# Moving a per-edge matrix product from the relation stage into the convolution stage of a graph network kernel

## The chip, the cores and the metric

VectorE (DVE) and ScalarE (ACT) do elementwise work, GpSimd (POOL) issues the indirect DMAs that gather rows by index, SyncE (SP) issues plain DMAs. Each engine works through its own list in order; semaphores order the engines among one another.

## The reference, cut to what matters

There are 6250 nodes with 128 features, and 100,000 edges sorted by target `dst`. Four graph layers run one after the other, each with its own weights and each followed by a residual and a normalization. Two of them matter here. They use the same edge features `edge_attr` (100,000 x 128).

```
layer 0 (convolution):
    h   = x @ w1.T + b1
    msg = silu(h[src] + (edge_attr @ we.T + be))
    agg = segment_sum(msg, dst)
layer 3 (relation network), the first linear layer of its edge MLP, 384 -> 256:
    hidden = relu(concat(h3[dst], h3[src], edge_attr) @ re_w1 + re_b1)
    effect = segment_sum(hidden @ re_w2 + re_b2, dst)
```

The kernel splits `re_w1` in three. The products of the node features with two of the parts are tables of 6250 rows, made once. The third product is `edge_attr @ re_w1[256:384]`, a 128 -> 256 product for every edge. It depends on inputs and weights alone. `re_w2` is applied after the sum over edges, in the update stage.

## The kernel before, in words

The edges lie in tiles of 128, one edge per partition. `G` = 4 tiles make a group, and four groups (`U` = 16 tiles) a round. The convolution's edge loop (`phase_conv_edges`) makes the messages of 196 groups of tiles, and sums them over 208 groups of steps. A step is a pair of an edge tile and a node tile that it touches; there are a few more steps than tiles. The relation's edge loop (`phase_relation`, after its node part) runs over 208 groups of steps. Each order is written out by hand: `staggered` and `pipeline` call each engine's stage functions turn by turn, with fixed lags in turns, and everything between engines is a wait on a counting semaphore.

Convolution, of one group n. SP loads 4 tiles of transposed edge features (`load`, L632). POOL issues 4 indirect DMAs, each gathering 128 rows of 512 bytes (L646), into one of 4 row buffers per group, when `row_free` says that the message four groups back is made (L742). PE multiplies the edge features with `we` into one PSUM bank (`edge_product`, L664, 4 products of 128 columns, each two matmul instructions). DVE adds the rows (`message`, L738) into a ring in SBUF, ACT applies SiLU in place (L689). For the sum over edges DVE compares the numbers 0 to 127 with each edge's target column (`one_hot`, L729, 128x512), PE multiplies that matrix with the messages (`sum_into_nodes`, L679), and DVE adds the four results to the node sums one after the other (`add_sums`, L760). Per turn DVE's order is match_high (L717, each fourth turn), one_hot(n), message(n), next_idx, add_sums(n-1), count_high (L724, each fourth turn). PE's order is edge_product(n), then sum_into_nodes(n-1), which waits until message(n) is made. Here `lane`, the row of numbers 0 to 127, is a copy in PSUM bank 7.

Relation, of one group n. SP loads 4 tiles of edge features again (L1583, 64 KB each) and the broadcast target columns (L1580). POOL gathers 4 times 128 rows of 1 KB (L1596). ACT makes the transposed one-hots in two steps, |rel - p| and then relu(1 - that) (`distance` L1647, `is_nought` L1654). PE accumulates two products in PSUM for each tile (`hidden_product`): edge features by `re_w1`'s third part (L1618) and one-hot by node table (L1619), 256 columns each. DVE adds the gathered rows in two halves (`add_rows`, L1710), ACT applies ReLU (`act`, L1659, 128x1024), DVE makes the one-hots for the sum (`sum_matrix`, L1699, two instructions of 128x256), PE sums (`sum_into_nodes`, L1630, 256 columns), DVE adds to the node sums (`add_sums`, L1731), and DVE casts the next indices (`stage`, L1670). `sum_matrix` of group n waits on `spread` until sum_into_nodes(n-2) has read that buffer of `oh`.

Of the kernel before, what the change touches and what calls it, by code (L numbers as in the profile page):

```python
# [21 lines left out]
F32 = mybir.dt.float32  # L22
# [582 lines left out]
def phase_conv_edges(nc, k, table, agg, room):  # L605

    with ExitStack() as c:
# [5 lines left out]
        ea = room[:, (RING + U) * D:(RING + 2 * U) * D].rearrange("p (j e) -> p j e", e=G * P)  # L613
        oh = sb("oh", [P, 2, G, P], F32)
        ea_in = [sem(f"ea_in{j}") for j in range(GROUPS)]
        row_in = k.row_in
        ea_free, row_free, idx_ready, pool_turn = sem("ea_free"), sem("row_free"), sem("idx_ready"), sem("pool_turn")
# [7 lines left out]
        lane, lane_set = k.psum[:, 7, 0:P], sem("lane_set")  # L625
        of_ring = lambda j: ring[:, G * j:G * j + G, :]
        with nc.Block() as block:
            @block.sync
            def _(sp):
                def load(i, j):  # L630
                    sp.wait_ge(ea_free, PER * i + j + 1)
# [3 lines left out]
                staggered(PER, (load, 0, TILE_GROUPS))  # L635
# [17 lines left out]
            def _(pe):  # L653
                pe.sem_inc(ea_free, GROUPS)
                pe.sem_inc(spread, 2)
                pe.matmul(lane, k.ident[:], k.lane[:], start=True, stop=True).then_inc(lane_set, 1)
                regs = {}

                def edge_product(i, j):
                    n = PER * i + j  # L660
                    pe.wait_ge(summed, n + 1)
                    pe.wait_ge(ea_in[j % GROUPS], 16 * (TURNS * i + j // GROUPS) + 16)
                    for q in range(G):
                        mm = pe.matmul(k.psum[:, j % 2, q * D:(q + 1) * D], ea[:, j % GROUPS, q * P:(q + 1) * P],  # L664
                                       k.w["L0_gnn_wet"][:], start=True, stop=True)
                    mm.then_inc(product, 1)
                    pe.wait_ge(product, n + 1)
                    pe.sem_inc(ea_free, 1)

                def sum_into_nodes(i, j):  # L670
# [4 lines left out]
                    pe.wait_ge(summed, min(n + 4, TILE_GROUPS + 2) if isinstance(n, int) else n + 4)  # L675
                    pe.wait_ge(oh_ready, n + 1)
                    pe.wait_ge(added, G * n + G)
                    for q in range(G):
                        mm = pe.matmul(k.psum[:, 2 + j % 2, q * D:(q + 1) * D], oh[:, j % 2, q, :],  # L679
# [6 lines left out]
            def _(a):  # L686
                def act(i, j):
                    a.wait_ge(summed, PER * i + j + 3)
                    nc.scalar.activation(of_ring(j), of_ring(j), ACT.Silu).then_inc(msg_ready, 1)  # L689

                staggered(PER, (act, 0, TILE_GROUPS))

            @block.vector
            def _(v):
                v.sem_inc(summed, 2)
# [15 lines left out]

                v.wait_ge(lane_set, 1)
# [20 lines left out]
                def message(i, j):  # L733
                    n = PER * i + j
                    v.wait_ge(product, n + 1)
                    for q in range(G):
                        v.wait_ge(row_in[G * (j % GROUPS) + q], 16 * (TURNS * i + j // GROUPS) + 16)
# [1294 lines left out]
```

## Time and profile before

| | us |
|---|---|
| median of 3 runs | 5034.16 (5031.56 to 5040.16) |
| the profiled execution | 5032.72 |
| its span, first to last instruction | 5030.9 |
| mean granted TensorE clock of the span | 0.781 |
| first and last gather of the convolution's edge loop (start) | 83.0, 1074.5 |
| first and last gather of the relation's edge loop (start) | 3803.0, 4887.1 |

The span is 1.8 us shorter than the profiled execution's time. The table's last two rows place the loops that are changed; the work between them (placing and attending by source, attention heads) is not changed in the code. Matmul ends are modelled, so a PE that shows as busy all the time isn't thereby at its limit; the rate of its instruction starts tells more.

### The profile page before, as it was taken

The numbers are of one execution on the slowest core, as the hardware profiler recorded it, in microseconds if no ns is written. First come the engines' busy times: TensorE is split into PE (matmuls) and PEld (weight loads), VectorE is DVE, ScalarE is ACT, GpSimd is POOL, SyncE is SP. The second block draws the span as 40 slices with busy tenths as digits, with TensorE's granted clock in tenths as the row PEclk, the third lists the DMA queues.
The fourth block names the chain that finished last, engine by engine and source line by source line (L and its number), as shares of the span: only waits on it lengthen the run. The fifth ranks groups of instructions, "written<-read, shape, count | busy, mean of one in ns | idle before, by whom it ended". The sixth has DMA issues, their size and how long they took to land. (4 is left out here: it accounts for less than half of the span.)

```text
span 5030.9 us, 76241 instructions
## 1 busy us (share of the span) xinstructions
PE 3877.7 (77%) x19917; PEld 3472.4 (69%) x19917; DVE 2952.5 (59%) x8048; ACT 1631.2 (32%) x2985; POOL 3439.9 (68%) x3536
## 2 busy tenths in 40 slices
PE   4556555555999999996986556566559999999998
PEld 3555555554988888886765555555548888888885
DVE  6555555557433333334786667667676666666665
ACT  1111111113333333334863233323325444444442
POOL 3777777742777777777645777777755777777761
PEclk7776777766665666557997777777779999999999
DMA  4333333327333333334754444444436666666651
GB/s 122 105 103 105 103 104 104 103 67 127 105 101 102 106 101 103 100 103 136 221 156 147 129 128 130 129 128 129 129 89 187 178 178 178 178 178 179 178 152 60
DMA packets 491437, 649.05 MB, mean 129 GB/s; under 512 B 94519, under 2 KB 354059, under 8 KB 490798
## 3 DMA queue, kind: packets, MB, share of 16 engines
q0 software_dynamic: 132032, 325.99, 22.5%
q1 hardware_dynamic: 346462, 312.02, 22.4%
q10 hardware_dynamic: 12560, 6.52, 0.8%
q8 instruction: 168, 2.75, 0.2%
q14 instruction: 215, 1.76, 0.1%
HBM read 554.38 MB, written 89.82 MB: 128 GB/s over the span
## 5 line engine op out<-in xcount | busy, mean ns | idle before, releaser
L1181 POOL DMA_INDIRECT by_src<-R,p_idx x832 | 833.3, 1002 | 345.1 <-issue 224.0
L1596 POOL DMA_INDIRECT R<-table_ps,r_idx x832 | 815.6, 980 | 339.6 <-issue 210.9
L1376 POOL DMA_INDIRECT R<-table_kv,h_idx x832 | 811.4, 975 | 322.3 <-issue 297.4
L646 POOL DMA_INDIRECT R<-table,c_idx x784 | 747.2, 953 | 275.5 <-issue 236.5
L1406 PE MATMUL psum<-R,h_oh 128*128 128x137 f32 x1664 | 357.3, 378 | 417.7 <-issue 235.8
L679 PE MATMUL psum<-R,c_oh 128*128 x1664 | 333.0, 362 | 421.3 <-DVE R L738 412.7
L1406 PEld LDWEIGHTS psum<-R,h_oh 128*128 128x128 f32 x1664 | 306.7, 265 | 459.3 <-issue 457.6
L679 PEld LDWEIGHTS psum<-R,c_oh 128*128 128x128 f32 x1664 | 281.6, 255 | 472.7 <-issue 472.7
L1731 DVE TENSOR_TENSOR R<-R,psum 128x256 f32 x832 | 345.9, 416 | 379.8 <-PE psum L1630 378.7
L760 DVE TENSOR_TENSOR R<-R,psum 128x128 f32 x832 | 238.8, 287 | 466.8 <-PE psum L679 372.5
L1618 PE MATMUL psum<-w_L_gnn_re_w,r_ea 128*128 128x256 f32 x1664 | 496.0, 380 | 2.5 <-issue 2.5
L1619 PE MATMUL psum<-R 128*128 x1664 | 495.6, 379 | 0.0
L984 PE MATMUL psum<-p_src_score,R 128*128 128x50 f32 x1664 | 450.1, 363 | 54.0 <-issue 53.8
L984 PEld LDWEIGHTS psum<-p_src_score,R 128*128 128x128 f32 x1664 | 363.0, 269 | 83.7 <-issue 83.7
L1659 ACT ACTIVATE X<-X 128x1024 f32<-128x1024 f32 x208 | 219.8, 1057 | 602.4 <-DVE X L1710 602.4
L689 ACT ACTIVATE R<-R 128x512 f32<-128x512 f32 x196 | 123.4, 629 | 884.9 <-DVE R L738 884.9
L1630 PE MATMUL psum<-X,early_cols 128*128 128x256 f32 x1664 | 393.0, 379 | 2.5 <-ACT X L1659 2.5
L985 PE MATMUL psum<-R 128*128 x1664 | 388.6, 303 | 0.0
L994 PE MATMUL psum<-R 128*128 x1664 | 381.7, 422 | 0.0
L1145 DVE SCALAR_TENSOR_TENSOR R<-early_cols,src_cols 128x8 f32<-128x8 f32 x104 | 18.6, 178 | 604.4 <-ACTq L1030 604.4
L985 PEld LDWEIGHTS psum<-R 128*128 128x128 f32 x1664 | 372.1, 275 | 0.0
L994 PEld LDWEIGHTS psum<-R 128*128 128x128 f32 x1664 | 361.3, 328 | 0.0
(337 smaller groups left out, 7773.6 us busy)
## 6 DMA issues: line engine op xcount, KB each, us to landing
R<-by_src SPq DMA_DIRECT2D x220, 260.0 KB, 3.1
r_ea<-in_ea_t SPq DMA_DIRECT2D x832, 64.0 KB, 2.8
R<-in_ea_t SPq DMA_DIRECT2D x196, 256.0 KB
R<-rel_rows SPq DMA_DIRECT2D x104, 256.0 KB
R<-lo_rows SPq DMA_DIRECT2D x104, 256.0 KB, 3.8
h_rel<-rel_rows SPq DMA_DIRECT2D x208, 128.0 KB, 3.1
r_rel<-rel_rows SPq DMA_DIRECT2D x208, 128.0 KB, 3.1
by_src<-R,p_idx POOLq DMA_INDIRECT x832, 2.5
```

What stands on the lines that cost most here:

```text
L646: g.indirect_dma_start(out=rows[:, u, :], out_offset=None, in_=table, in_offset=bass.IndirectOffsetOnAxis(ap=idx[:, j // GROUPS % 2, u:u + ...
L679: mm = pe.matmul(k.psum[:, 2 + j % 2, q * D:(q + 1) * D], oh[:, j % 2, q, :], ring[:, bass.ds(regs["slot"][G * (j % GROUPS) + q], 1), :], ...
L984: pe.matmul(cols[:, 0:NT], is_lo[:, j, q * P:(q + 1) * P], src_score[:], start=True, stop=True)
L985: mm = pe.matmul(cols[:, NT:WIDE], is_rel[:, j, q * P:(q + 1) * P], H[:, bass.ds(regs["node"][G8 * j + q], 1), D + 1:D + 2], start=True, s ...
L994: mm = pe.matmul(k.psum[:, 4 + 2 * j + h, (q % G) * D:(q % G + 1) * D], is_rel[:, j, q * P:(q + 1) * P], H[:, bass.ds(regs["node"][G8 * j ...
L1181: g.indirect_dma_start(out=by_src, out_offset=bass.IndirectOffsetOnAxis(ap=idx[:, u:u + 1], axis=0), in_=rows[:, u, :], in_offset=None).th ...
L1376: g.indirect_dma_start(out=rows[:, u, :], out_offset=None, in_=table, in_offset=bass.IndirectOffsetOnAxis(ap=idx[:, u:u + 1], axis=0)).the ...
L1406: mm = pe.matmul(sums(j, q), oh[:, j % 2, q, :], msg[:, j % 2, q, :], start=True, stop=True)
L1596: g.indirect_dma_start(out=rows[:, u, :], out_offset=None, in_=table, in_offset=bass.IndirectOffsetOnAxis(ap=idx[:, u:u + 1], axis=0)).the ...
L1618: pe.matmul(hidden(j, q), ea[:, G * j + q, :], k.w["L3_gnn_re_w1"][:, 2 * HID:3 * HID], start=True, stop=False)
L1619: mm = pe.matmul(hidden(j, q), oht[:, j % 2, q * P:(q + 1) * P], Dh[:, bass.ds(regs["node"][G * j + q], 1), :], start=False, stop=True)
L1630: mm = pe.matmul(sums(j, q), oh[:, j % 2, q, :], msg[:, j % 2, q, :], start=True, stop=True)
```

## The change

The convolution's PE product gets a moving operand of 384 columns (`both`): `re_w1`'s third part and `we` side by side. Of each tile it makes 256 columns of the relation's edge product and 128 of the convolution's, in one bank. A group takes two halves of two banks, and three such pairs of banks rotate (`of_banks`); the banks 6 and 7 hold the sums, and so `lane` is now read from SBUF. DVE makes the message in two halves. ACT copies each half's 256 columns from PSUM into `part` in SBUF (`keep`), then applies SiLU. SP stores `part` to DRAM (`store`, 512 KB per group) in a new tensor `edge_part`.

The relation loads 128 KB of `edge_part` per tile in place of 64 KB of edge features. DVE adds the gathered rows to it in SBUF (`join`, two halves), and `add_rows` adds the PSUM product to that sum. PE's `hidden_product` has the one-hot product alone. `sum_matrix` moves from DVE to ACT, as four |.| of 128x128 and a relu of 128x512. The size of the scratch memory for dynamic DMAs is given as 8192 at the build, where it was left to the default.

```diff
@@ phase_conv_edges
+        both = room[:, used:used + HID + D]
+        of_banks = lambda h, cols: k.psum[:, 2 * (h % 3):2 * (h % 3) + HALF, cols]
-        lane, lane_set = k.psum[:, 7, 0:P], sem("lane_set")
+        lane = k.lane[:]
 sync:
+                def store(i, j):
+                    n = PER * i + j
+                    sp.wait_ge(kept, 2 * n + 5)
+                    sp.dma_start(k.edge_part[n * G * P:(n + 1) * G * P, :].rearrange("(q p) d -> p q d", p=P), part[:, j % GROUPS]
+                                 ).then_inc(part_out[j % GROUPS], 16)
-                staggered(PER, (load, 0, TILE_GROUPS))
+                staggered(PER, (load, 0, TILE_GROUPS), (store, GROUPS, TILE_GROUPS))
 tensor, edge_product:
-                    pe.wait_ge(summed, n + 1)
-                    for q in range(G):
-                        mm = pe.matmul(k.psum[:, j % 2, q * D:(q + 1) * D], ea[:, j % GROUPS, q * P:(q + 1) * P],
-                                       k.w["L0_gnn_wet"][:], start=True, stop=True)
+                    for h in (2 * n, 2 * n + 1):
+                        pe.wait_ge(kept, h + 1)
+                        for q in range(HALF):
+                            at = (h % 2 * HALF + q) * P
+                            mm = pe.matmul(k.psum[:, 2 * (h % 3) + q, 0:HID + D], ea[:, j % GROUPS, at:at + P], both,
+                                           start=True, stop=True)
+                        mm.then_inc(product, 1)
 scalar:
+                def keep(i, j):
+                    turn = TURNS * i + j // GROUPS
+                    if turn > 0:
+                        a.wait_ge(part_out[j % GROUPS], 16 * turn)
+                    for h in range(2):
+                        n = 2 * (PER * i + j) + h
+                        a.wait_ge(summed, n + 1)
+                        nc.scalar.copy(part[:, j % GROUPS, h * HALF:h * HALF + HALF], of_banks(n, slice(0, HID))).then_inc(kept, 1)
 vector, message:
+                    for h in (2 * n, 2 * n + 1):
+                        v.wait_ge(product, h + 1)
+                        v.tensor_tensor(of_ring(j)[:, at:at + HALF, :], of_banks(h, slice(HID, HID + D)), rows[:, u:u + HALF, :],
+                                        ALU.add).then_inc(summed, 1)
@@ phase_relation
 sync:
-                            sp.wait_ge(product, GROUPS * i + j + 1)
+                            sp.wait_ge(summed, 2 * (GROUPS * i + j) + 2)
-                        sp.dma_start(ea[:, u, :], k.ea_t[:, bass.ds(tile[u] * P, P)]).then_inc(ea_in[u], 16)
+                        sp.dma_start(part[:, u, :], k.edge_part[bass.ds(tile[u] * P, P), :]).then_inc(part_in[j], 16)
 gpsimd:
-                            g.wait_ge(summed, 2 * (GROUPS * i + u // G) + 2)
+                            g.wait_ge(joined, 2 * (GROUPS * i + u // G) + 2)
 tensor, hidden_product:
-                        pe.matmul(hidden(j, q), ea[:, G * j + q, :], k.w["L3_gnn_re_w1"][:, 2 * HID:3 * HID], start=True, stop=False)
 scalar:
+                def sum_matrix(i, j):
+                    n = GROUPS * i + j
+                    a.wait_ge(spread, n + 1)
+                    for q in range(G):
+                        at = i * U + G * j + q
+                        nc.scalar.activation(oh[:, j % 2, q, :], k.lane[:], ACT.Abs, bias=k.rel_cols[:, at:at + 1],
+                                             scale=-1.0).then_inc(sum_apart, 1)
+                    a.wait_ge(sum_apart, G * n + G)
+                    nc.scalar.activation(oh[:, j % 2], oh[:, j % 2], ACT.Relu, bias=k.ones[:, 0:1], scale=-1.0).then_inc(oh_ready, 1)
-                pipeline(ITERS, GROUPS, distance, is_nought, act, lags=(0, 1, 3))
+                pipeline(ITERS, GROUPS, distance, is_nought, sum_matrix, act, lags=(0, 1, 2, 3))
 vector:
+                def join(h):
+                    def join_half(i, j):
+                        u = G * j + 2 * h
+                        if h == 0:
+                            v.wait_ge(part_in[j], 16 * G * (i + 1))
+                        for q in range(2):
+                            v.wait_ge(row_in[u + q], 16 * i + 16 * (before + 1))
+                        v.tensor_tensor(part[:, u:u + 2, :], part[:, u:u + 2, :], rows[:, u:u + 2, :], ALU.add).then_inc(joined, 1)
+                        if h == 1:
+                            stage(i + 1, j)
+                    return join_half
-                pipeline(ITERS, GROUPS, add_sums(0), sum_matrix, add_sums(1), add_rows(0), add_sums(2),
-                         add_rows(1), add_sums(3), lags=(3, 1, 3, 1, 3, 1, 3))
+                pipeline(ITERS, GROUPS, add_sums(0), join(0), add_sums(1), join(1), add_sums(2), add_rows(0), add_sums(3),
+                         add_rows(1), lags=(3, 1, 3, 1, 3, 1, 3, 1))
@@ build
-    nc = bacc.Bacc("TRN2", target_bir_lowering=False, num_devices=1)
+    nc = bacc.Bacc("TRN2", target_bir_lowering=False, num_devices=1, dynamic_dma_scratch_size=8192)
```

## Rows read from the trace of the kernel before

**Rows 1.** Windows: busy us and instructions per engine, clock, DMA share, GB/s.
```profile
500.00:625.00 125.00, 72.70 (x387) 66.86 (x388) 67.46 (x165) 15.74 (x25) 94.83 (x100) 0.72 0.38 105
2375.00:2500.00 125.00, 113.85 (x828) 99.86 (x827) 99.59 (x311) 105.86 (x413) 85.18 (x104) 1.00 0.80 221
2875.00:3000.00 125.00, 72.80 (x397) 66.93 (x398) 87.09 (x249) 38.67 (x75) 95.32 (x98) 0.78 0.47 129
4250.00:4375.00 125.00, 125.00 (x581) 110.04 (x580) 80.47 (x216) 55.44 (x74) 95.73 (x97) 1.00 0.62 178
```

**Rows 2.** Groups of instructions, convolution, 82 to 1122: busy us, mean ns | idle before.
```profile
L646 POOL DMA_INDIRECT R<-table,c_idx x784 | 747.2, 953 | 275.5 <-issue 236.5 <-DVE c_idx L700 30.2 <-DVEq L742 8.8
...
L760 DVE TENSOR_TENSOR R<-R,psum 128x128 f32 x827 | 237.4, 287 | 465.7 <-PE psum L679 372.0 <-DVE R L760 3.7 <-issue 3.2
L729 DVE TENSOR_TENSOR c_oh<-psum,rel_cols 128x512 f32<-128x512 f32 x208 | 141.9, 682 | 0.4
L738 DVE TENSOR_TENSOR R<-psum,R 128x512 f32<-128x512 f32 x196 | 133.4, 681 | 6.9 <-DMA R<-table,c_idx 6.9
...
L724 DVE TENSOR_REDUCE count<-c_same_high 128x7 f32<-128x896 bf16 x49 | 52.9, 1080 | 0.0
```

**Rows 3.** Line L738 (message): ns min/median/max, first and last start.
```profile
L738 DVE TENSOR_TENSOR R<-psum,R x196: 674/681/693, 90.4 to 1089.8; 128x512 f32<-128x512 f32 x196
```

**Rows 4.** Line L646 (gather), and what its engine sat idle for (us, times).
```profile
L646 POOL DMA_INDIRECT R<-table,c_idx x784: 946/952/1730, 83.0 to 1074.5; - x196
...
  DVEq L742: 8.8, 27
```

**Rows 5.** Timeline, convolution, TensorE at the upper clock: start us, us.
```profile
612.52 0.68 DVE L738 TENSOR_TENSOR R<-psum,R 128x512 f32<-128x512 f32 x1
...
613.40 1.15 PE L679 MATMUL psum<-R,c_oh 128*128 x8 [2.23 <-DVE R L738]
...
614.70 1.58 DVE L760 TENSOR_TENSOR R<-R,psum 128x128 f32 x4 [1.50 <-PE psum L679]
```

**Rows 6.** Timeline, convolution, the same product at the lower clock.
```profile
603.68 2.07 PE L679 MATMUL psum<-R,c_oh 128*128 x8 [1.78 <-DVE R L738]
```

**Rows 7.** Timeline, relation, a turn in the steady stretch.
```profile
4300.56 0.68 DVE L1710 TENSOR_TENSOR X<-psum,R 128x512 f32<-128x512 f32 x1
...
4301.28 1.06 ACT L1659 ACTIVATE X<-X 128x1024 f32<-128x1024 f32 x1 [2.90 <-DVE X L1710]
4301.43 1.89 PE L1630 MATMUL psum<-X,early_cols 128*128 128x256 f32 x8
...
4302.85 0.70 ACT L1654 ACTIVATE R<-R,ones 128x512 f32<-128x512 f32 x1
...
4303.47 0.42 DVE L1731 TENSOR_TENSOR R<-R,psum 128x256 f32 x1 [1.83 <-PE psum L1630]
...
4303.81 0.76 DVE L1699 TENSOR_TENSOR early_cols<-lane,rel_cols 128x256 f32<-128x256 f32 x2
...
4304.26 1.12 POOL L1596 DMA_INDIRECT R<-table_ps,r_idx  x1 [0.30 <-issue]
...
4305.68 0.95 POOL L1596 DMA_INDIRECT R<-table_ps,r_idx  x1 [0.30 <-issue]
...
4306.41 0.41 DVE L1731 TENSOR_TENSOR R<-R,psum 128x256 f32 x1
...
4306.61 1.89 PE L1630 MATMUL psum<-X,early_cols 128*128 128x256 f32 x8
```

**Rows 8.** Groups of instructions, POOL in the heads stage, 2800 to 3700.
```profile
L1376 POOL DMA_INDIRECT R<-table_kv,h_idx x704 | 686.7, 975 | 214.5 <-issue 191.9 <-DVE h_idx L1449 22.5
```

**Rows 9.** Timeline, ACT in the attend stage: a |.| of 128x128 and its follower.
```profile
2479.72 0.39 ACT L1240 ACTIVATE a_away<-lane,R 128x128 f32<-128x128 f32 x1
2480.01 0.19 ACT L1234 ACTIVATE a_minus<-a_weight 128x1 f32<-128x1 f32 x1
```

**Rows 10.** Groups of instructions, ACT, whole span: a copy of 128x512 from PSUM.
```profile
L1033 ACT COPY R<-psum 128x512 f32<-128x512 f32 x208 | 112.8, 590 | 731.3 <-DMA by_src<-R,p_idx 607.5 <-PE psum L994 123.8
```

More of the change, by code:

```diff
@@ L613, in phase_conv_edges @@
         ea = room[:, (RING + U) * D:(RING + 2 * U) * D].rearrange("p (j e) -> p j e", e=G * P)
+        used = (RING + 2 * U) * D
+        part = room[:, used:used + GROUPS * G * HID].rearrange("p (j q d) -> p j q d", j=GROUPS, d=HID)
+        used += GROUPS * G * HID
+        both = room[:, used:used + HID + D]
+        kept, both_ready, part_out = sem("kept"), sem("both_ready"), [sem(f"part_out{j}") for j in range(GROUPS)]
+        HALF = G // 2
+        of_banks = lambda h, cols: k.psum[:, 2 * (h % 3):2 * (h % 3) + HALF, cols]
         oh = sb("oh", [P, 2, G, P], F32)
@@ L653, in _ @@
             def _(pe):
-                pe.sem_inc(ea_free, GROUPS)
                 pe.sem_inc(spread, 2)
-                pe.matmul(lane, k.ident[:], k.lane[:], start=True, stop=True).then_inc(lane_set, 1)
+                pe.wait_ge(both_ready, 2)
                 regs = {}
@@ L1551, in phase_relation @@
         oh = k.early_cols[:, 0:2 * G * P].rearrange("p (b q e) -> p b q e", b=2, q=G)
-        ea_in = [sem(f"ea_in{u}") for u in range(U)]
+        part = sb("part", [P, U, HID], F32)
+        part_in = [sem(f"part_in{j}") for j in range(GROUPS)]
+        joined, sum_apart = sem("joined"), sem("sum_apart")
         rel_in = [sem(f"rel_in{n}") for n in range(GROUPS)]
@@ L1665, in _ @@
                 v.sem_inc(summed, 2 * GROUPS)
+                v.sem_inc(joined, 2 * GROUPS)
                 v.sem_inc(spread, 2)
@@ L1694, in _ @@
                 v.wait_ge(zeroed, 1)
[L1696 to L1702 removed]
+                def join(h):
[9 more added lines that the diff above has]
+                    return join_half
                 def add_rows(h):
                     def add_half(i, j):
+                        n = GROUPS * i + j
+                        u = G * j + 2 * h
                         if h == 0:
[L1707 to L1709 removed]
+                            v.wait_ge(product, n + 1 + GROUPS)
+                        v.wait_ge(joined, 2 * (n + GROUPS) + h + 1)
                         v.tensor_tensor(msg[:, j % 2, 2 * h:2 * h + 2, :].rearrange("p q d -> p (q d)"),
                                         k.psum[:, 2 * (j % 2) + h, :],
[L1712 removed]
+                                        part[:, u:u + 2, :].rearrange("p q d -> p (q d)"),
                                         ALU.add).then_inc(summed, 1)
[L1714 to L1716 removed]
                     return add_half
```

59 lines of the change are left out of this document (22 added, 37 removed).

## The prediction

> **What bounds the kernel now.** I read first which engine is full in which stretch (busy time by windows), then each changed loop's costliest groups, then one turn of each loop in the timeline.
>
> The two loops have different bounds. In the relation TensorE's clock is granted in full and it shows as busy throughout [rows 1]. From one sum product to the next are 4306.61 - 4301.43 = 5.18 us [rows 7]. Eight instructions of 256 columns take 1.89 us to the last one's end [rows 7]; with one instruction's 0.38 us taken off, that is 1.51 / 7 = 0.216 us from start to start. A turn has 24 of them, 5.18 us. So PE is the bound there, and POOL is close behind: a gather lasts 0.95 us with 0.30 us before it, so four of them take 5.02 us, and 5.2 with the longer one of 1.12 us [rows 7].
>
> In the convolution PE is busy 73 of 125 us and POOL 95 [rows 1], which looks like a POOL bound. The loop's own rates say something finer. Messages are made every (1089.8 - 90.4) / 195 = 5.13 us [rows 3]. Gathers would go every 5.02 us by the same 0.95 + 0.30 [rows 2], and they do (1074.5 - 83.0) / 783 x 4 = 5.07 us only because POOL waits at times for a row buffer that VectorE gives back [rows 4]. At the end the last message starts 1089.8 - 1074.5 - 0.95 = 14.3 us behind the last gather. So the bound is a loop of DVE and PE: message(n), PE's sum product, four dependent additions, one-hot, message(n+1). At the upper clock the step through PE costs 1.50 us, at the lower one PE's part is 2.07 instead of 1.15 [rows 5, 6]. The mean clock is 0.72 [rows 1]. POOL is 0.1 us per group faster than this loop, no more.
>
> **Convolution, after.** PE's work grows. The new product has 384 columns, so 0.216 x 1.5 = 0.324 us per instruction, 2.6 us for the eight of a group, beside about 0.9 us for the sum. That is 3.5 of some 5.1 us. At the lower clock it would be 7.0 us, which doesn't fit, so PE would never rest and would be back at the upper one. Does the upper one hold at 68%? The attend stage has 828 instructions in 125 us at some 0.11 us each (eight of 128 columns in 1.15 us less the last one's own end [rows 5]), 73%, and shows a clock of 1.00 [rows 1]. I take 1.00.
>
> The DVE loop then is 1.50 (PE step) + 1.58 (four additions) + 0.27 (a quarter of count_high's 1.08) + 0.68 (one-hot) + 0.33 and 0.42 (the message's halves, priced as the 128x256 additions of the relation) = 4.8 us [rows 2, 5, 7]. By PE it is 0.2 + 0.9 + 2.6 + 0.2 + 0.42 = 4.3 us. Both are under POOL's 5.02, so POOL becomes the bound. ACT's two copies of 128x512 from PSUM at 0.59 [rows 10] and the SiLU make 1.8 us per group, beside everything; three pairs of banks let PE run ahead of them. The store waits on `kept`, on SP, with only a load behind it that is due three groups later; nothing waits for it but `keep` four groups on. It adds 512 KB per 5.1 us, 100 GB/s to 105. DMA share goes from 0.38 to perhaps 0.7, and 0.80 has been carried [rows 1]. Cost zero, plus some 3 us for the last stores' landing.
>
> POOL doesn't stay at 5.02, however. The one-hot now reads `lane` in SBUF, so both its inputs lie there. In the relation a gather that starts at 4304.26, under L1699 with both inputs in SBUF (4303.81 to 4304.57), lasts 1.12 us where the next takes 0.95 [rows 7]. The gather waits until that instruction ends. In the heads stage, with one such instruction of 128x512 in each group, gathers have a mean of 975 ns against 953 here [rows 2, 8]. The bounds: no hit, 5.02 us per group; a hit of the full 0.6 us in each group, 5.6. I take the heads' rate, a start every 1.28 us. The last gather starts at 83.0 + 783 x 1.28 = 1085, is done by 1086 and lands some 2 us later, so the last message starts at 1088 instead of 1089.8: -2 us. With the store +1 us. Ends: at 1.255 us it would be 83 + 983 + 3 = 1069, -21 us; at 1.40 us 1182, +92 us.
>
> The Trainium skill (SBUF — State Buffer, Who interferes with whom) has a rule for this: a VectorE instruction with two SBUF inputs contends with a GpSimd instruction that reads SBUF, and the second to issue is blocked until the first is done. The row above agrees in that the gather is the longer one. The same page infers that descriptor generation isn't held by `tensor_tensor`; by that the convolution would gain the 21 us, and the 1.12 us speaks against it.
>
> **Relation, after.** PE loses 8 of 24 instructions: 16 x 0.216 = 3.45 us per turn. POOL's floor is 5.02, DVE's turn is 4306.41 + 0.41 - 4303.47 = 3.35 us of work now [rows 7], less two halves of 128x256 (0.67) plus two joins of 128x512 (2 x 0.6): 3.9. ACT gets four |.| and a relu of 0.70. The |.| of the same form lasts 0.39 and the next instruction starts 0.29 after its start [rows 9], so four take 3 x 0.29 + 0.39 = 1.26. ACT's sum is 2 x 0.61 + 1.26 + 0.1 + 0.70 + 0.96 = 4.2 us. Each engine alone has room.
>
> What has none is a new ring. sum_matrix(n+1) on ACT waits for `spread` of sum_into_nodes(n-1). Behind it in ACT's order stands act(n), and sum_into_nodes(n) waits for act(n). Before, `sum_matrix` was on DVE; act(n), at 4301.28 to 4302.34, ended 4.3 us ahead of its product at 4306.61 [rows 7]. Now each turn has in series: PE's eight products 1.89; to ACT 0.15 (as PE to DVE, 4303.32 to 4303.47); |.| 1.26; wait for the last one 0.1; relu 0.70; act 1.06 less 0.1 of overlap; to PE 0.2: 5.26 us [rows 5, 7, 9]. That is over PE's old 5.18 and over POOL. distance and is_nought (1.3) run beside PE's 1.89, hidden_product (1.7) beside ACT's 3.0. The bounds: |.| as close as its data alone allow and no hand-over cost gives 4.9, under POOL, so 5.02 and (5.02 - 5.18) x 208 = -33 us; 0.39 each for |.| and slow hand-overs 5.6, +87 us. I take 5.26: +0.08 x 208 = +17 us. Under this ring POOL has 0.24 us per turn to spare for the joins, both of whose inputs lie in SBUF; a hit on one of four gathers costs about that much, so it is free at best just so. SP's loads double to 512 KB per turn, some 220 GB/s, at a share near 0.8; they are asked for four turns ahead, as the buffer is free after add_rows. I price them at zero.
>
> **The smaller scratch for DMAs.** No row shows its cost. The bounds are nothing and, were each of 3280 gathers and scatters held by a hundredth of a microsecond or two, some 50 us. The 0.30 between gathers is the same everywhere, and no wait for room is seen. I take zero.
>
> **Sum.** 5032.7 (this execution) + 1 + 17 = 5051 for the profiled execution. The median shown is 1.4 us above it: 5052. The first product of the convolution now stands behind two copies on ACT, and the relation's last ones behind one more |.| and relu (1.26 + 0.70): with 4 us for these, 5056. A difference of 0.2% (10 us) is about what a measurement tells from none.
>
> **Rivals.**
> A, both loops at POOL's pace without hits: the ring closes in under 5.02, one-hot and joins fall between gathers. -21 + 3 - 33 = -51 from the median: 4983. For it: each engine's sum is below 5.02 and the gather grid can lock to the DVE order. Against it: the series on ACT, and the 1.12. A half of it (one loop) gives 5015. Chance 0.28 together.
> B, the hits decide (the other side of A): in the relation two joins of 0.6 us under four gather starts give 2 x 0.6 / 5.2 x 4 = 0.9 hits of 0.3 us or more, 5.33 us; in the convolution the one-hot hits once per group, 5.3. (5.33 - 5.18) x 208 + 196 x 0.2 = +31 + 39: 5105. It decides once POOL is behind the ring, from 0.24 us of hits per turn. Chance 0.2.
> C, PE's clock falls in the new idle third: the convolution has 36% of PE's time in use at the upper clock and swings between both levels (mean 0.72). If relation and convolution came to 0.85, the ring would have 1.9 more in a third of turns: +0.6 x 208, 5180. Against it the attend stage. Chance 0.05.
> D, the ring costs just what PE cost, and the rest cancels: 5034, within 10 us. Chance 0.17. My forecast, 5056, has 0.3.
> Faster 0.29, same 0.21, slower 0.5. The range is 4990 to 5120; it leaves out the best of A and C.
>
> **What would show it.** Relation: sum products 5.26 us apart, ACT busy over 4 us a turn, ACT's idle time before sum_matrix ended by PE's sum product, and that product waiting on ACT's act; POOL waiting on the cast. If PE waits on DVE, and DVE on gathers, it is B. Convolution: message waits for rows and the lag behind the gathers stays near 2 us; gathers over 0.95 us under the one-hot; clock near 1.0. I'm wrong if either loop gets shorter by over 10 us (now 991.5 us from the convolution's first to last gather start [rows 4], some 208 x 5.18 in the relation), or if a stage that isn't changed gets longer (the scratch).

## The result and the profile after

The changed kernel takes 5006.00 us (median of 4 runs, 4999.22 to 5011.64) against 5034.21 before. The ratio is 0.9945, with a 95% interval of 0.9933 to 0.9957: it is 0.55% faster, where 5056 us and the range 4990 to 5120 had been forecast. The time lies in the range, on the wrong side of before.

First the windows of the changed kernel, in the convolution and in the relation; the columns are those of [rows 1].

```profile
500.00:625.00 125.00, 93.09 (x386) 57.76 (x385) 69.02 (x187) 39.22 (x72) 95.13 (x99) 0.97 0.67 203
4250.00:4375.00 125.00, 91.42 (x395) 72.75 (x394) 95.94 (x222) 102.84 (x196) 94.84 (x100) 1.00 0.80 234
```

In the convolution the granted clock went from 0.72 to 0.97 [rows 1], and the DMAs' share to 0.67 at 203 GB/s. In the relation PE fell from 125 to 91 us in 125, and ACT rose from 55 to 103. Now the lines of the convolution's messages and gathers, first and last start, as in [rows 3, 4].

```profile
L767 DVE TENSOR_TENSOR R<-psum,R x392: 406/418/426, 88.4 to 1089.7; 128x256 f32<-128x256 f32 x196
```

```profile
L663 POOL DMA_INDIRECT R<-table,c_idx x784: 947/952/1726, 83.6 to 1084.4; - x196
...
  DVEq L770: 7.0, 23
```

The last message starts at 1089.7 us, before at 1089.8 [rows 3]. So the convolution as a whole came out even. But it goes by another engine now: the last message follows the last gather by 4.4 us (1089.7 - 1084.4 - 0.95) where it was 14.3 us behind, and the gathers themselves take 9.3 us more from first to last (1000.8 against 991.5). The gathers' groups in the whole span, busy us, mean ns:

```profile
L1404 POOL DMA_INDIRECT R<-table_kv,h_idx x832 | 811.5, 975 | 324.4 <-issue 301.6
L1625 POOL DMA_INDIRECT R<-table_ps,r_idx x832 | 801.4, 963 | 324.1 <-issue 192.6
L663 POOL DMA_INDIRECT R<-table,c_idx x784 | 763.2, 973 | 268.7 <-issue 231.6
```

The convolution's gather has a mean of 973 ns instead of 953 [rows 2], as forecast (975); the heads stage's is the same as before [rows 8]. The relation's gather got shorter, which nothing in the prediction says. Before it was:

```profile
L1596 POOL DMA_INDIRECT R<-table_ps,r_idx x832 | 815.6, 980 | 339.6 <-issue 210.9 <-DMA table_ps<-R 70.2 <-DVE r_idx L1670 58.5
```

The gain is in the relation. Its sum products, first and last start:

```profile
L1656 PE MATMUL psum<-X,early_cols x1664: 378/379/635, 3831.3 to 4879.4; 128*128 128x256 f32 x185
```

Eight of them are a turn, so a turn takes (4879.4 - 3831.3) / 1663 x 8 = 5.042 us in the mean. The kernel before in the same view:

```profile
L1630 PE MATMUL psum<-X,early_cols x1664: 379/379/483, 3835.2 to 4904.9; 128*128 128x256 f32 x185
```

That is 5.146 us. The difference is 0.104 x 208 = 21.6 us; with a first sum product 3.9 us earlier, the last one comes 25.5 us earlier. The span is 27.1 us shorter (5003.8 against 5030.9). In the column "turn" below it is this figure throughout: last less first start of the sum product's matmuls, by 1663, by 8. It is good for differences between kernels of one pace, but it reads low, as the loop's last turns are cut short, and it reads lowest where POOL sets the pace: there the sum products begin some 25 us behind the first gather and end close behind the last. So the column "steady" has the pace in the middle of the loop, from the sum product of turn 20 to that of turn 180, by 160. Before it is 5.180 us, just the 5.18 that the prediction took from one turn [rows 7], and in the changed kernel 5.064.

One turn in the timeline shows what ends it: start us, us.

```profile
4302.20 1.99 PE L1656 MATMUL psum<-X,early_cols 128*128 128x256 f32 x8 [1.34 <-ACT X L1695]
...
4304.23 1.28 ACT L1688 ACTIVATE early_cols<-lane,rel_cols 128x128 f32<-128x128 f32 x4 [0.86 <-PE psum L1656]
...
4305.55 0.72 ACT L1691 ACTIVATE early_cols<-early_cols,ones 128x512 f32<-128x512 f32 x1
...
4306.17 1.04 ACT L1695 ACTIVATE X<-X 128x1024 f32<-128x1024 f32 x1
...
4307.27 1.99 PE L1656 MATMUL psum<-X,early_cols 128*128 128x256 f32 x8 [1.34 <-ACT X L1695]
```

This is the ring of the prediction, closed: products, four |.|, relu, act, products, in 5.07 us. Each step starts 0.04 to 0.06 us after the one in front of it has ended, and act 0.1 us before the relu's end. And the waits between 3830 and 4870 us (us, times, longest) say that it is so in every turn:

```profile
PE psum L1656 <- ACT X L1695: 275.6, 206, 1.3
DVE R L1770 <- PE psum L1656: 241.4, 205, 2.1
POOL R L1625 <- issue: 187.1, 613, 0.7
ACT early_cols L1688 <- PE psum L1656: 176.9, 205, 1.5
POOL R L1625 <- DVE r_idx L1707: 61.0, 200, 0.3
```

PE waits for act 206 times, ACT for the products 205 times. POOL waits for the cast 200 times, but 0.3 us at most, and that is what lies between two gathers anyway: POOL is level with the ring.

### The profile page after: what moved, and what is told of

It is laid out like the page before. It is cut to its first block and busy times, and to the rows that moved or that the text cites. A ratio compares the mean times of both kernels' runs of the same rounds, so it can differ in the third digit from the quotient of the medians.

```text
span 5003.8 us, 74941 instructions
## 1 busy us (share of the span) xinstructions
PE 3708.8 (74%) x18251; PEld 3049.6 (61%) x18251; DVE 3087.5 (62%) x8244; ACT 2222.8 (44%) x4419; POOL 3445.2 (69%) x3536
## 5 line engine op out<-in xcount | busy, mean ns | idle before, releaser
L1209 POOL DMA_INDIRECT by_src<-R,p_idx x832 | 836.7, 1006 | 342.4 <-issue 222.2
L1625 POOL DMA_INDIRECT R<-table_ps,r_idx x832 | 801.4, 963 | 324.1 <-issue 192.6
L663 POOL DMA_INDIRECT R<-table,c_idx x784 | 763.2, 973 | 268.7 <-issue 231.6
L1656 PE MATMUL psum<-X,early_cols 128*128 128x256 f32 x1664 | 416.2, 393 | 278.7 <-ACT X L1695 278.7
L682 PE MATMUL psum<-R 128*128 128x384 f32 x1568 | 557.2, 500 | 13.3 <-DMA R<-in_ea_t 13.3
L1656 PEld LDWEIGHTS psum<-X,early_cols 128*128 128x128 f32 x1664 | 300.5, 190 | 394.4 <-ACT X L1695 361.8
L714 ACT COPY R<-psum 128x512 f32<-128x512 f32 x392 | 216.6, 587 | 686.9 <-DVE R L767 680.8
L695 PEld LDWEIGHTS psum<-R,c_oh 128*128 128x128 f32 x1664 | 214.3, 201 | 379.8 <-issue 379.8
L695 PE MATMUL psum<-R,c_oh 128*128 x1664 | 254.8, 299 | 257.5 <-issue 248.8
L1061 ACT COPY R<-psum 128x512 f32<-128x512 f32 x208 | 112.4, 590 | 735.0 <-DMA by_src<-R,p_idx 638.4
L682 PEld LDWEIGHTS psum<-R 128*128 128x128 f32 x1568 | 293.6, 198 | 179.1 <-issue 31.1
L1646 PE MATMUL psum<-R 128*128 x1664 | 394.4, 380 | 2.6 <-issue 2.6
L1013 PE MATMUL psum<-R 128*128 x1664 | 385.0, 301 | 0.0
L1022 PE MATMUL psum<-R 128*128 x1664 | 380.7, 422 | 0.0
```

The costliest lines, as they stand in the source:

```text
L663: g.indirect_dma_start(out=rows[:, u, :], out_offset=None, in_=table, in_offset=bass.IndirectOffsetOnAxis(ap=idx[:, j // GROUPS % 2, u:u + ...
L682: mm = pe.matmul(k.psum[:, 2 * (h % 3) + q, 0:HID + D], ea[:, j % GROUPS, at:at + P], both, start=True, stop=True)
L695: mm = pe.matmul(k.psum[:, 6 + j % 2, q * D:(q + 1) * D], oh[:, j % 2, q, :], ring[:, bass.ds(regs["slot"][G * (j % GROUPS) + q], 1), :], ...
L1013: mm = pe.matmul(cols[:, NT:WIDE], is_rel[:, j, q * P:(q + 1) * P], H[:, bass.ds(regs["node"][G8 * j + q], 1), D + 1:D + 2], start=True, s ...
L1022: mm = pe.matmul(k.psum[:, 4 + 2 * j + h, (q % G) * D:(q % G + 1) * D], is_rel[:, j, q * P:(q + 1) * P], H[:, bass.ds(regs["node"][G8 * j ...
L1209: g.indirect_dma_start(out=by_src, out_offset=bass.IndirectOffsetOnAxis(ap=idx[:, u:u + 1], axis=0), in_=rows[:, u, :], in_offset=None).th ...
```

## The experiments

| run | us | ratio to before, interval | turn | steady | clock, 4250 to 4375 |
|---|---|---|---|---|---|
| changed kernel | 5006.0 | 0.9945 (0.9933 to 0.9957) | 5.042 | 5.064 | 1.00 |
| e1 convolution changed only | 5038.0 | 1.0006 (0.9996 to 1.0015) | 5.146 | 5.180 | 1.00 |
| e2 two more in the ring | 5202.9 | 1.0327 (1.0310 to 1.0344) | 5.956 | 5.998 | 0.92 |
| e3 act first | 5036.3 | 0.9999 (0.9989 to 1.0009) | 5.147 | 5.217 | 0.99 |
| e4 act first, two more | 5027.7 | 0.9990 (0.9981 to 1.0000) | 5.116 | 5.169 | 0.97 |
| e5 before, no edge product | 4991.9 | 0.9924 (0.9908 to 0.9941) | 5.007 | 5.076 | 1.00 |
| e6 one-hots on DVE | 5037.7 | 1.0016 (1.0006 to 1.0026) | 5.172 | 5.238 | 0.96 |
| e7 wide product alone | 5015.2 | 0.9970 (0.9958 to 0.9983) | 5.146 | 5.180 | 1.00 |
| e8 narrow product alone | 5043.4 | 1.0033 (1.0021 to 1.0044) | 5.146 | 5.180 | 1.00 |
| e9 two pairs of banks | 5012.8 | 0.9964 (0.9951 to 0.9976) | 5.036 | 5.064 | 1.00 |
| e10 lane in PSUM | 4994.1 | 0.9922 (0.9905 to 0.9938) | 5.047 | 5.063 | 1.00 |
| e11 lane in PSUM, act first | 5015.3 | 0.9966 (0.9956 to 0.9976) | 5.150 | 5.217 | 0.97 |
| e12 scratch only | 5034.0 | 1.0005 (0.9995 to 1.0014) | 5.146 | 5.180 | 1.00 |
| e13 act first, no join | 4981.3 | 0.9900 (0.9883 to 0.9916) | 4.928 | 5.002 | 0.95 |
| e14 ring, no join | 5008.4 | 0.9945 (0.9929 to 0.9962) | 5.042 | 5.063 | 1.00 |
| e15 two more, warm | 5137.1 | 1.0209 (1.0192 to 1.0227) | 5.626 | 5.647 | 1.00 |
| e16 act first, warm | 5034.8 | 1.0007 (0.9997 to 1.0017) | 5.154 | 5.180 | 1.00 |

Each group of runs had the kernel before measured beside it, which took 5028.7 to 5034.2 us (medians). So times in us are compared within a group (e1 to e4, e5 to e8, e9 to e12, e13 to e16), and ratios across groups; 0.001 is 5 us.

**Which stage gained: e1 and e12.** In e1 the convolution is the changed one, with its stores, and `phase_relation` is taken whole from the kernel before.

> The convolution of the changed kernel, with its stores of the edge products, before the relation of the old one (edge features loaded, both products on TensorE, one-hots on VectorE); the scratch is the small one. Theory T (the whole gain is the relation's, the convolution comes out even): 5034, within 8 us, the relation's sum products 5.16 us apart on average. Rival (the warm TensorE clock of the convolution gives part of the gain): 5015 to 5024.

Measured 1.0006, turn 5.146, as before. All of the gain is the relation's. e12 changes one argument of the kernel before:

```diff
-    nc = bacc.Bacc("TRN2", target_bir_lowering=False, num_devices=1)
+    nc = bacc.Bacc("TRN2", target_bir_lowering=False, num_devices=1, dynamic_dma_scratch_size=8192)
```

> The kernel before with the smaller scratch for dynamic DMAs alone. It costs nothing: within 3 us of before, all gathers as long as before. Rival: held gathers, +10 us or more, spread over all four gather stages.

Measured 1.0005. The smaller scratch costs nothing that can be told.

**Whether the ring paces the relation: e2, e3, e4.** Two more |.| go ahead of the four (their output is used by nothing):

```diff
+                    for q in range(2):
+                        nc.scalar.activation(spare[:, U * HID + 4 * G * P + q * P:][:, 0:P], k.lane[:], ACT.Abs, bias=k.minus_part[:, 0:1],
+                                             scale=-1.0).then_inc(sum_apart, 1)
                     for q in range(G):
-                    a.wait_ge(sum_apart, G * n + G)
+                    a.wait_ge(sum_apart, (G + 2) * (n + 1))
```

> The changed kernel with two more |.| of 128x128 on ScalarE in each sum_matrix, ahead of the four; their output isn't used. Theory T (the relation goes by a ring through ScalarE and TensorE: sum_matrix, act, sum product): a turn gets 2 x 0.29 = 0.58 us longer, 5.07 to 5.65, 208 x 0.58 = +121 us over the changed kernel's 5006: 5127. Rival P (the relation goes by GpSimd's gathers, ScalarE has slack at 103 of 125 us): +0 to +20 us.

and act goes before sum_matrix (e3; e4 has both edits):

```diff
-                pipeline(ITERS, GROUPS, distance, is_nought, sum_matrix, act, lags=(0, 1, 2, 3))
+                pipeline(ITERS, GROUPS, distance, is_nought, act, sum_matrix, lags=(0, 1, 3, 2))
```

> The changed kernel, with act placed before sum_matrix in ScalarE's order, so that sum_matrix(n+1) no longer stands in front of act(n). Theory T: the ring is gone and GpSimd is next, at 5.02 us plus hits of the joins; a turn of 5.02 to 5.07, 0 to -10 us against the changed kernel, ScalarE no longer waits for TensorE in each turn. Rival P: no change at all.

> Both edits: act first, and two more |.| in each sum_matrix. Theory T: without the ring the extra 0.58 us has room (ScalarE's sum is some 4.8 us of 5.02), so within 10 us of the kernel with act first alone, and over 100 us below the one with two more in the ring. Rival (ScalarE's whole work is what counts, not the ring): +100 us or more here too.

e2 is 0.038 above the changed kernel in the ratio, 192 us, more than the 121 of a ring. e4 isn't slower than e3 by the same two instructions: its median is 9 us lower, but the intervals overlap. So ACT's sum isn't the bound, its order is: the ring paces. But e3 itself contradicts what I expected of it. Without the ring the kernel is not 0 to 10 us faster but slower by 0.0054 in the ratio, 27 us, though nothing on ACT or PE paces the turn any more. Its waits in the relation, 3860 to 4880 us:

```profile
PE psum L1646 <- DVE X L1752: 250.9, 162, 3.8
POOL R L1625 <- issue: 216.9, 711, 0.3
DVE r_part L1740 <- DMA R<-table_ps,r_idx: 204.2, 279, 3.1
...
POOL R L1625 <- DVE r_idx L1707: 21.6, 71, 0.3
```

The join (L1740) now waits for gathered rows, 279 times; in the changed kernel it never did. POOL itself waits for nothing longer than its 0.3 us between gathers, so POOL is the bound: a turn is four gathers and four such gaps. And its gathers are longer:

```profile
L1625 POOL DMA_INDIRECT R<-table_ps,r_idx x832 | 832.5, 1001 | 326.2 <-issue 231.2 <-DMA table_ps<-R 72.7 <-DVE r_idx L1707 22.3
```

1001 ns in the mean against 963: (1001 - 963) x 832 = 32 us, and by the steady turn (5.217 - 5.064) x 208 = 32 us too; the kernel lost 27. That was an argument at this point; e13 and e14 test it.

**Whether the joins hold the gathers: e13, e14, e16.** The stored edge product is loaded but not added, so its share is missing from the result; `add_rows` reads the gathered rows and casts the next indices. e13 has act first, e14 keeps the ring.

```diff
-                        v.tensor_tensor(part[:, u:u + 2, :], part[:, u:u + 2, :], rows[:, u:u + 2, :], ALU.add).then_inc(joined, 1)
-                        v.wait_ge(joined, 2 * (n + GROUPS) + h + 1)
+                        for q in range(2):
+                            v.wait_ge(row_in[u + q], 16 * i + 16 * (before + 1))
-                                        part[:, u:u + 2, :].rearrange("p q d -> p (q d)"),
+                                        rows[:, u:u + 2, :].rearrange("p q d -> p (q d)"),
-                            g.wait_ge(joined, 2 * (GROUPS * i + u // G) + 2)
+                            g.wait_ge(summed, 2 * (GROUPS * i + u // G) + 2)
```

> act before sum_matrix, and without the joins: the stored edge product is loaded but not added (its share is missing), add_rows reads the gathered rows. No VectorE instruction of the relation has two SBUF inputs any more. Theory L (with act first GpSimd is the bound, and the joins hold its gathers: 43 us of excess over 832 gathers): gather mean 1001 down to about 950 ns, a turn of 5.02 to 5.04, 22 us or more below act first alone (5036), near 5010. Rival K (the order on ScalarE or TensorE's clock made act first slow): it stays at 5.1 or more per turn.

> The changed kernel without the joins, ring kept. Theory L (the ring paces the turn at 5.04 and keeps gathers and joins out of each other's way): gathers a little shorter, the turn unchanged, within 5 us of the changed kernel. Rival (the joins cost here too): a turn of 5.02 or less, 5 to 15 us faster.

e16 has act first, keeps the joins and gives PE its 24 instructions per turn back:

```diff
+                        for again in range(2):
                             mm = pe.matmul(hidden(j, q), oht[:, j % 2, q * P:(q + 1) * P],
```

> act before sum_matrix, each hidden product made twice. With act first the clock was 0.97 in the relation. Theory L (the joins' hits): no gain, a turn of 5.13 or more. Rival K2 (the clock's dips made act first slow): a turn under 5.08 at clock 1.00.

The gathers of e13, then the two that ring and joins leave:

```profile
L1625 POOL DMA_INDIRECT R<-table_ps,r_idx x832 | 786.4, 945 | 329.9 <-issue 230.0 <-DMA table_ps<-R 72.7 <-DVE r_idx L1707 27.2
```

```profile
L1625 POOL DMA_INDIRECT R<-table_ps,r_idx x832 | 786.2, 945 | 340.8 <-issue 246.2 <-DMA table_ps<-R 72.7 <-DVE r_idx L1707 22.0
```

The second is e14's. With act first the joins' absence brings gathers from 1001 to 945 ns and the time from a ratio of 0.9999 to 0.9900, 50 us: theory L, and more than the 22 us asked of it. The edit takes work off DVE as well, but POOL, the bound, didn't wait for DVE in e3. With the ring (e14) gathers get shorter too, by 18 ns, but the turn stays at 5.042 and the ratio at 0.9945: the ring paces, and has room for these holds. The clock didn't make act-first slow: e13 has a lower one than e3 (0.95 against 0.99) and is the faster. (Its gathers start at 3801.2 to 4843.9 us, every 1042.7 / 831 x 4 = 5.02 us; the turn of 4.93 is below that because the first sum products come late and the last ones right behind their gathers.)

e16 can't tell about the clock, though it was built for that. Its window:

```profile
4250.00:4375.00 125.00, 125.00 (x581) 110.32 (x580) 94.10 (x219) 103.34 (x193) 95.10 (x97) 1.00 0.78 229
```

PE is busy throughout with the same 581 instructions as in the kernel before [rows 1], and the steady turn is 5.180 in both. The doubled product has made PE the bound again, so theory and rival ask for the same here: a turn under 5.08 was out of reach whatever the clock did.

The gathers one by one say what the joins do to them. First the changed kernel, then e3:

```profile
4304.68 0.68 DVE L1740 TENSOR_TENSOR r_part<-r_part,R 128x512 f32<-128x512 f32 x1
...
4305.18 1.01 POOL L1625 DMA_INDIRECT R<-table_ps,r_idx  x1 [0.30 <-issue]
```

```profile
4330.48 0.69 DVE L1740 TENSOR_TENSOR r_part<-r_part,R 128x512 f32<-128x512 f32 x1 [0.87 <-DMA R<-table_ps,r_idx]
...
4330.58 1.42 POOL L1625 DMA_INDIRECT R<-table_ps,r_idx  x1 [0.30 <-issue]
```

A gather that starts while a join runs is longer, one that starts at another time isn't. In the changed kernel 199 of the 832 gathers start under a join, about one per turn, with 0.20 us of it left in the mean; they take 1.02 us, all others 0.95. In e3 it is about as often, 215, but with 0.34 us left, and they take 1.15. The excess is what is left of the join less 0.13 us, in the changed kernel and (under the one-hots) in the kernel before.

So the ring does two things. It paces a turn, at 5.064 us, and it fixes where in a turn the joins meet a gather: at their end, for 0.06 us. Four gathers of 0.945 with their gaps take 5.00 us (e13: 5.002), so 0.06 is just what the ring leaves POOL. Left to run at its own pace POOL meets the joins anywhere and is slower than the ring: 5.217.

**What the ring costs beyond its sum: e15.** Two more |.| in the ring, and the doubled product of e16.

> Two more |.| in the ring, and each hidden product made twice, so TensorE again has 24 instructions per turn (the second overwrites the first). With two more |.| alone the turn took 5.96 us where 5.63 had been forecast, at a granted clock of 0.91. Theory W (the clock fell because TensorE rested, and the slower products lengthened the ring): clock 1.00, a turn of 5.62 to 5.7, over 40 us faster than without the doubled product. Rival (the two |.| cost more than 0.58 by themselves): no faster than 5.9 per turn.

PE in e2, with no doubled product, start us, us:

```profile
4404.75 1.99 PE L1656 MATMUL psum<-X,early_cols 128*128 128x256 f32 x8 [1.41 <-ACT X L1698]
...
4410.40 1.99 PE L1656 MATMUL psum<-X,early_cols 128*128 128x256 f32 x8 [1.93 <-ACT X L1698]
...
4416.05 1.99 PE L1656 MATMUL psum<-X,early_cols 128*128 128x256 f32 x8 [1.93 <-ACT X L1698]
...
4421.69 3.03 PE L1656 MATMUL psum<-X,early_cols 128*128 128x256 f32 x8 [1.93 <-ACT X L1698]
...
4428.38 1.99 PE L1656 MATMUL psum<-X,early_cols 128*128 128x256 f32 x8 [1.28 <-ACT X L1698]
```

and the window 4250 to 4375 in e2 and in e15:

```profile
4250.00:4375.00 125.00, 87.85 (x335) 68.77 (x335) 81.56 (x189) 99.45 (x210) 79.51 (x84) 0.92 0.67 199
```

```profile
4250.00:4375.00 125.00, 120.51 (x531) 99.34 (x532) 86.14 (x199) 105.37 (x223) 84.07 (x89) 1.00 0.70 210
```

Where the products take 1.99 us, e2's turns are 5.65 us, the 5.07 + 0.58 asked of them. Its mean of 5.96 comes from turns like the one from 4421.69, whose products take 3.03 us and which lasts 6.69; the granted clock is 0.92 in the mean. With the doubled product the clock is 1.00, the steady turn 5.647 and the mean one 5.626. So some 60 us of e2's loss are the clock's (the ratios 1.0327 and 1.0209, by 5034).

**What the relation's parts were worth: e5, e6.** e5 is the kernel before without the first of the two products (its share is missing):

```diff
-                        pe.matmul(hidden(j, q), ea[:, G * j + q, :], k.w["L3_gnn_re_w1"][:, 2 * HID:3 * HID], start=True, stop=False)
                         mm = pe.matmul(hidden(j, q), oht[:, j % 2, q * P:(q + 1) * P],
-                                       Dh[:, bass.ds(regs["node"][G * j + q], 1), :], start=False, stop=True)
+                                       Dh[:, bass.ds(regs["node"][G * j + q], 1), :], start=True, stop=True)
```

> The kernel before with the relation's edge product left out of TensorE (8 of 24 matmul instructions of a turn; its share of the sum is missing); loads, one-hots on VectorE and all else stay. Theory T (TensorE's 24 instructions were the bound): a turn falls from 5.16 to GpSimd's pace, 5.02 plus the hits of the one-hots, 5.02 to 5.1: -12 to -29 us. Rival (GpSimd with its one long gather per turn was as much the bound): 5.15 or more, within 5 us of before.

e6 is the changed kernel with sum_matrix as VectorE had it, at the end of its turn:

```diff
-                pipeline(ITERS, GROUPS, distance, is_nought, sum_matrix, act, lags=(0, 1, 2, 3))
+                pipeline(ITERS, GROUPS, distance, is_nought, act, lags=(0, 1, 3))
-                         add_rows(1), lags=(3, 1, 3, 1, 3, 1, 3, 1))
+                         add_rows(1), sum_matrix, lags=(3, 1, 3, 1, 3, 1, 3, 1, 1))
```

> The changed kernel with the relation's one-hots for the sum back on VectorE, at the end of its turn. Theory T: no ring through ScalarE; VectorE's work is 3.9 + 0.7 = 4.6 us plus its wait for the sum product, and three instructions kinds with two inputs in SBUF hit the gathers: a turn of 5.05 to 5.2, 0 to +27 us against the changed kernel. Rival (the move to ScalarE costs more in its ring than it saves): a turn under 5.05, faster than the changed kernel.

e5: ratio 0.9924, a turn of 5.007 us and a steady one of 5.076. PE was the bound, and POOL with its holds (a gather mean of 963 ns) was next. The first product out of PE gains 37 us on its own before (5028.7), over the 12 to 29 asked; the turns explain 29 of them, and why the relation also starts 13.5 us earlier in this execution is open. e6: 1.0016, a steady turn of 5.238, at a gather mean of 1006 ns, with two kinds of instructions on VectorE that have two SBUF inputs, joins and one-hots (my expectation said three). It is 0.0071 above the changed kernel, 36 us, where at most 27 were asked. But beside e3 (5.217, 1001 ns) it lost 0.02 us per turn, and the ratios' intervals (1.0006 to 1.0026, 0.9989 to 1.0009) touch: one-hots off DVE were worth next to nothing by themselves. What the move to ScalarE gained came through the ring that I had priced as its cost.

**How the convolution came out even: e7, e8, e9, e10.** e7 and e8 have the old relation and neither copies nor stores; the message is made in halves, in two pairs of banks, and `lane` is in PSUM as before. They differ in one line, here from e8 to e7:

```diff
-                            mm = pe.matmul(k.psum[:, 2 * (h % 2) + q, HID:HID + D], ea[:, j % GROUPS, at:at + P], both[:, HID:HID + D],
+                            mm = pe.matmul(k.psum[:, 2 * (h % 2) + q, 0:HID + D], ea[:, j % GROUPS, at:at + P], both,
```

> Relation as before. The convolution makes the product of 384 columns, but 256 of them are neither copied nor stored; message in two halves, two pairs of banks, lane in PSUM as before. Theory C (TensorE's clock set the pace of the old convolution, more work lifts it): clock about 1.0, messages at GpSimd's 5.02, last message some 20 us earlier: 5010 to 5018. Rival (more TensorE work only costs): slower than before, 5040 or more.

> The same, with the product of 128 columns alone: what the halves, the banks and the small scratch do by themselves. Theory C: clock 0.72 as before, messages every 5.1 to 5.2 us, 5034 to 5045, 15 us or more over the wide one. Rival: as fast as the wide one, so the order and the halves did it and not the clock.

The messages of e7, then its window 500 to 625, and then the same two of e8:

```profile
L753 DVE TENSOR_TENSOR R<-psum,R x392: 405/414/426, 88.4 to 1072.2; 128x256 f32<-128x256 f32 x196
```

```profile
500.00:625.00 125.00, 93.10 (x400) 58.05 (x399) 70.68 (x193) 15.75 (x25) 94.82 (x100) 1.00 0.38 105
```

```profile
L753 DVE TENSOR_TENSOR R<-psum,R x392: 405/412/425, 87.8 to 1105.7; 128x256 f32<-128x256 f32 x196
```

```profile
500.00:625.00 125.00, 73.34 (x384) 67.47 (x384) 68.14 (x187) 15.11 (x24) 91.71 (x98) 0.71 0.37 102
```

Three times the columns in the edge product, and the kernel is 28 us faster (5015.2 against 5043.4; the last message 33.5 us earlier). The code differs in the columns alone, and the clock is 1.00 instead of 0.71. The message in halves, with its banks and waits, costs some 16 us at that low clock (e8's 1105.7 against 1089.8 [rows 3]); at the full one the loop goes by the gathers, (1068.1 - 83.1) / 783 x 4 = 5.03 us in e7, and no price of the halves is seen. e9 is the changed kernel with two pairs of banks (and the semaphore counts that go with them):

```diff
-        of_banks = lambda h, cols: k.psum[:, 2 * (h % 3):2 * (h % 3) + HALF, cols]
+        of_banks = lambda h, cols: k.psum[:, 2 * (h % 2):2 * (h % 2) + HALF, cols]
```

> The changed kernel with two pairs of product banks in the convolution in place of three. Both theories: nothing, within 3 us of the changed kernel, since a pair is copied out half a turn before it is due.

e10 is e9 with `lane` in a freed bank:

```diff
-        lane = k.lane[:]
+        lane, lane_set = k.psum[:, 4, 0:P], sem("lane_set")
```

> Two pairs of banks, and the freed bank holds lane, so the convolution's one-hot has one input in SBUF. Theory H (gathers that start under an instruction with both inputs in SBUF are held until it ends, and the changed convolution goes by the gathers): gather mean 973 back to 953 ns, 784 x 0.02 = -16 us against two pairs alone, messages 5.03 us apart. Rival (the convolution still goes by VectorE's loop): gathers 953 ns, time the same within 3 us.

The messages of e9 and of e10:

```profile
L767 DVE TENSOR_TENSOR R<-psum,R x392: 406/418/426, 88.3 to 1091.0; 128x256 f32<-128x256 f32 x196
```

```profile
L770 DVE TENSOR_TENSOR R<-psum,R x392: 407/415/426, 88.2 to 1076.3; 128x256 f32<-128x256 f32 x196
```

The third pair of banks did nothing: e9's last message is 1.3 us from the changed kernel's, and the intervals of their ratios overlap. `lane` in PSUM brings the gather mean from 976 to 957 ns and the last message 14.7 us forward; the time falls by 18.8 us, as theory H had it (16). The gathers one by one agree: 86 of the changed kernel's 784 start under a one-hot with both inputs in SBUF and take 1.12 us in the mean, and in the kernel before 98 start under a one-hot that reads `lane` in PSUM and take 0.95.

So the convolution came out even by two effects of one size. The clock brought the last message from 1089.8 to 1072.2 us (e7), and the changed kernel gave that back, 14.7 of the 17.5 us through the place of `lane`.

**The two edits together: e11.** 

> lane in PSUM in the convolution and act before sum_matrix in the relation. The two stages don't meet: the sum of what the two edits gave alone. With 16 us from the first and 0 to 10 from the second 4980 to 4990.

It kept the convolution's gain and lost the relation's (turn 5.150, gather mean 1001 ns as in e3): 5015.3, where 4980 to 4990 had been expected. The fastest kernel that makes the whole computation is e10, at 0.9922 (0.9905 to 0.9938), 18.8 us below e9, which is the changed kernel but for a pair of banks.

## Why the prediction was wrong

**The bound before** was read rightly in both loops: PE in the relation (e5), at 5.18 us a turn, and DVE and PE at a mixed clock in the convolution (e8 to e7).

**The convolution** was forecast at +1 us and came out at 0 by its last message, and by the steps that I had given: clock about 1.0 (0.97), POOL as the bound, gathers held by the one-hot (973 ns; I had taken 975), the last gather at 1084.4 (1085). e7 and e10 show that both effects were real. The copies and stores together can have cost little: e10, which has them, makes its last message 4.1 us after e7, which hasn't.

**The relation, the step that failed.** "Now each turn has in series ... 5.26 us. That is over PE's old 5.18." The ring is there, and it sets the turn, as said. Its length was mis-sized. The work in it was priced a little low: 1.89 + 1.26 + 0.70 + 1.06 = 4.91 less 0.1 forecast, 1.99 + 1.28 + 0.72 + 1.04 = 5.03 less 0.1 measured. The term that failed is the hand-overs. From PE to ACT, from the last |.| to the relu and from ACT to PE they were priced at 0.15 + 0.1 + 0.2 = 0.45 us, the first and the last from rows of TensorE and VectorE [rows 5, 7] and the middle one from no row; they are 0.04 + 0.04 + 0.06 = 0.14. That is 5.07 in place of 5.26, and the sign of the answer hung on it, with the old bound 0.08 us away at 5.18. Forecast +17 us, measured -21.6. The prediction had named a relation that gets shorter by over 10 us as a sign of being wrong, and that is what came.

That the joins cost nothing was forecast for a ring with 0.24 us to spare for POOL. The real one leaves 0.06, and the joins cost nothing even so (e14), since their meeting with the gathers shrank to just that. The forecast came true there by luck. Also, of [rows 7] I had said that the gather waits until the VectorE instruction ends: 0.31 us of it were left at 4304.26, and the gather was 0.17 longer. The first 0.13 us of a gather's issue aren't held.

**The rivals.** A came nearest: the half of it, one loop at POOL's pace, stood at 5015, and the relation took that pace within 0.06 us. Its condition failed all the same, as the ring doesn't close in under 5.02 and a gather per turn is held; nor did the convolution lose its holds. B, the hits, was right as a mechanism and wrong in its condition: the ring keeps the meetings short (e14), and without it B comes true (e3, 5.22 where I had 5.33). C, the clock, didn't come in the changed kernel (1.00), but it did in e2 (0.92). D, 5034, was 28 us off. The smaller scratch costs nothing that shows (e12).

**The Trainium skill's rule** (SBUF — State Buffer, Who interferes with whom), that a VectorE instruction with two SBUF inputs contends with a GpSimd instruction that reads SBUF, held: with such instructions in the relation gathers are longer by 18 to 56 ns in the mean, and with none no gather is (945 ns, at most 962, e13 and e14). The same section of the Trainium skill infers that descriptor generation isn't held by `tensor_tensor`; the gather's instruction on GpSimd, which issues it, is held here, up to 1.47 us in e3, and these runs don't tell which part of it.

## What to carry to other kernels

When a step moves to another engine, write down the ring it closes through that engine's order, and price its hand-overs from rows of the same pair of engines; where the answer hangs on a tenth of a microsecond per turn, the chance belongs near even. A TensorE that looks half idle may be slow for that reason: here more work on it made the stage faster. And before a ring is taken out, ask what it holds in step.

## What the runs showed of the hardware

- TensorE with three times the columns in one of its products ran a stage 33.5 us faster, since the granted clock rose from 0.71 to 1.00 (e8, e7). In the relation it stayed at 1.00 in the changed kernel and was 0.92 with two more |.| on ScalarE, which made TensorE wait longer in each turn (1.93 us where it had been 1.34; e2).
- A gather's issue on GpSimd takes 945 ns in the relation (e14) and is held when it starts under a VectorE instruction with two SBUF inputs, by what is left of that one less 0.13 us: a mean of 963 ns in step with them, 1001 out of step (changed kernel, e3). An operand moved to PSUM takes the hold away (976 to 957 ns, e10).
- From TensorE to ScalarE a hand-over shows as 0.04 us in the changed kernel's records and back as 0.06 (matmul ends are modelled).
- At a DMA share of 0.76 to 0.81 the relation's gathers land 3.5 to 4.3 us after their issue in the median (e16, e6, e4, e3, e13, e11, e9), at 0.62 to 0.63 in 3.0 to 3.6 (e7, e12, e8, e1), between these in 3.4 and 4.0 (e15, e2). In the changed kernel no join waited for them; where POOL paces, the joins do (e3).
